# A causal attention layer and a ternary feed-forward layer on one core: own instruction orders for the first two units and the last one, pairwise layer norms, and TensorE transposes of the last unit's probabilities

## What is computed

```python
def _L0_attn_ref(x, W_Q, W_K, W_V, W_O):
    q = jnp.einsum('bsd,hed->bhse', x, W_Q)
    k = jnp.einsum('bsd,hed->bhse', x, W_K)
    v = jnp.einsum('bsd,hed->bhse', x, W_V)
    scores = jnp.einsum('bhse,bhme->bhsm', q, k) * scale
    scores = jnp.where(causal, jnp.float32(-1000000000.0), scores)
    pattern = jax.nn.softmax(scores, axis=-1)
    z = jnp.einsum('bhsm,bhme->bhse', pattern, v)
    out = jnp.einsum('bhse,hde->bsd', z, W_O)
    return out
...
        scale = jnp.mean(jnp.abs(w))
        return jnp.clip(jnp.round(w / (scale + Q_EPS)), -1.0, 1.0)
...
    xn = layernorm(x, ln_gamma, ln_beta)
    w_q = ternary_quantize(weight)
    return jnp.einsum('bsi,oi->bso', xn, w_q) + bias
...
x = x + _L0_attn_ref(_layernorm(x, axis=-1), L0_attn_W_Q, L0_attn_W_K, L0_attn_W_V, L0_attn_W_O)
x = x + _L0_ffn_ref(_layernorm(x, axis=-1), L0_ffn_weight, L0_ffn_bias, L0_ffn_ln_gamma, L0_ffn_ln_beta)
```

## Time and profile before

| what | us |
|---|---|
| median of 3 runs | 897.38 |
| lowest, highest | 896.47, 899.69 |
| profiled execution, device time | 896.73 |
| its span | 894.4 |
| busy PE, DVE, ACT, POOL | 820.2, 673.1, 544.9, 548.8 |

### The profile page before, as it was taken

How to read it: one execution, slowest core, us unless ns; L and a number is a source line. 1 busy time by engine, 2 the same in 40 slices (tenths; PEclk the granted TensorE clock), 3 DMA queues, 4 the chain that set the end, 5 groups by cost and what they waited for, 6 DMA issues and landing times.

```text
span 894.4 us, 14482 instructions
## 1 busy us (share of the span) xinstructions
PE 820.2 (92%) x4790; PEld 731.5 (82%) x4790; DVE 673.1 (75%) x1448; ACT 544.9 (61%) x986; POOL 548.8 (61%) x283
## 2 busy tenths in 40 slices
PE   3879999999999999999999999999999999985264
PEld 3768889899988888888898998888888899974254
DVE  7577787877787787787877787787788777875444
ACT  1456666766666766666766766666667766654300
POOL 5026866677656855696577855684677666644521
PEclk7999999999999999999999999999999999998676
DMA  5045565566556565566555656556456655565011
GB/s 170 1 115 133 131 165 129 134 144 168 132 133 144 141 152 129 121 143 162 132 132 142 168 137 142 124 137 161 115 127 146 143 133 132 133 139 121 21 48 47
DMA packets 58696, 114.62 MB, mean 128 GB/s; under 512 B 17408, under 2 KB 21632, under 8 KB 58624
## 3 DMA queue, kind: packets, MB, share of 16 engines
q1 hardware_dynamic: 58624, 113.71, 53.2%
HBM read 10.88 MB, written 2.10 MB: 15 GB/s over the span
## 4 chain that ended last, share of the span: by engine, by line
PE 79%; DVE 7%; SPq 5%; DMA 3%; ACT 3%; issue 1%; POOL 1%; ACTq 0%; DVEq 0%
PE ring L460 21%; PE scores L498 20%; PE ring L439 17%; PE ring L448 9%; PE ring L469 9%; SPq L316 5%; DMA pT<-turn 3%; DVE norm L728 1%; PE ring L478 1%; DVE stats L710 1%; ACT turn L574 1%; POOL pT L383 1%; DVE scores L656 1%; PE ring L430 1%; ACT pT L594 1%
## 5 line engine op out<-in xcount | busy, mean ns | idle before, releaser
L383 POOL TENSOR_TENSOR pT<-pT 128x1024 fp32r<-128x1024 f32 x192 | 458.4, 2406 | 288.5 <-ACT pT L594 288.1
L656 DVE CUSTOM_DVE_ANT_0 scores<-scores,mask 128x128 f32<-128x128 f32 (+7 forms) x256 | 194.6, 760 | 157.3 <-PE scores L498 155.7
L574 ACT ACTIVATE turn<-scores,negmax 128x128 f32<-128x128 f32 (+7 forms) x256 | 189.4, 740 | 169.0 <-DMA pT<-turn 86.9
L498 PE MATMUL scores<-kT,qT 128*128 128x512 f32 (+3 forms) x1152 | 236.1, 344 | 11.7 <-ACT turn L574 10.1
L460 PE MATMUL ring<-pT,v 128*128 128x512 f32 (+3 forms) x1152 | 223.3, 348 | 9.4 <-POOL pT L383 9.4
L460 PEld LDWEIGHTS ring<-pT,v 128*128 128x128 f32 x1152 | 196.9, 190 | 39.1 <-issue 9.6
L594 ACT ACTIVATE pT<-pT 128x1024 fp32r<-128x1024 f32 x192 | 201.8, 1058 | 24.0 <-DMA pT<-turn 23.0
L498 PEld LDWEIGHTS scores<-kT,qT 128*128 128x128 f32 x1152 | 187.3, 190 | 34.1 <-ACT turn L574 14.1
L664 DVE STREAM_TRANSPOSE turn<-turn 128x128 f32<-128x128 f32 (+7 forms) x256 | 193.9, 768 | 2.3 <-ACT turn L574 2.2
L469 PE MATMUL ring<-wo_s,zT 128*128 128x256 f32 x768 | 114.7, 286 | 0.0
L439 PE MATMUL ring<-xT,wk_s 128*128 128x512 f32 x384 | 102.9, 404 | 8.9 <-DVE xT L752 7.8
(11 more groups left out here) (62 smaller groups left out, 462.7 us busy)
## 6 DMA issues: line engine op xcount, KB each, us to landing
pT<-turn SPq DMA_DIRECT2D x512, 128.0 KB, 2.3
pT<-turn SPq DMA_DIRECT2D x512, 64.0 KB, 2.0
acc<-in_x SPq DMA_DIRECT2D x4, 512.0 KB, 5.8
wq_raw<-in_wq SPq DMA_DIRECT2D x8, 256.0 KB, 3.6
wk_raw<-in_wk SPq DMA_DIRECT2D x8, 256.0 KB, 3.0
...
```

Source lines behind the costliest of these rows:

```text
L383: pool.tensor_tensor(chunk(half, LO, c), f32(chunk(half, LO, c)), f32(chunk(half, HI, c)), ALU.subtract).then_inc(plo_ready, 1)
L498: mm = pe.matmul(scores[:, t % 2, first + c:first + c + n], qT[:, par, a, t * P:(t + 1) * P], kT[:, par, m, c:c + n], start=(i == 0), stop ...
L574: act.activation(turn[half][:, :, 0:t + 1, q, :].rearrange("p b j i -> p j b i"), scores[:, t % 2, score_columns(t)].rearrange("p (j b i) ...
L656: dve.tensor_tensor_reduce(out=tile, in0=tile, in1=mask[:, S - (t + 1) * P:S], scale=-1.0, scalar=FAR, op0=ALU.add, op1=ALU.min, accum_out ...
```

## The change

The tables for the steady part are the same. `stream` is replaced by `run_of`, which runs a start list written out item by item (units 0 and 1), the table for units 2 to 30, and an end list written out item by item (from `pv` of unit 29 on). The rest:

- **Norms by pairs.** x is loaded, and both norms are worked, by pairs of tiles. For the first norm ScalarE writes the normed tiles (`Identity` with scale and bias), for which VectorE makes `-mean*rstd` (`shift`). In the second norm GpSimd writes pairs 0 to 3 and ScalarE pairs 4 to 7. An `x` or `xf` job is the four transposes of a pair. Two `ACT_TABLE_LOAD`s come in on ScalarE around the last exponentials.
- **Start.** GpSimd clears `turn1` before its weight splits and the k weights come first; `qk` 0 of units 0 and 1 are made together; the `wo` load waits for `x` 6 in place of the eighth group of transposes.
- **Last unit (31).** There is no flip, wave, `hip` or `lop`. Its exponentials go to `turn` in plain order (`last_turn`), TensorE transposes them by blocks of 128 x 128 in ten jobs `tp` (`TURNS`, 36 transposes), and ScalarE and VectorE split these into places of `xT`, `v`, `qT` and `kT` that are free by then (`last_probs`). The product with V is three jobs `pvl`, of query tiles 0 to 3, 4 and 5, 6 and 7 (`GROUPS`).
- **Second layer.** The ternary weight is made by GpSimd in three instructions (it was two on VectorE); the bias is added by pairs on GpSimd; `xf` and `ff` go pair by pair between the `o` jobs of unit 31.

```diff
+STEADY_FROM = 2
...
+        yield from start
+        for u in range(STEADY_FROM, LAST):
+            for entry in table:
+                item = entry[:-1] + (u + entry[-1],)
+                if exists(item):
+                    yield item
+        yield from end
...
+            def normalise(item):
+                kind, c = item
+                act.wait_ge(ln_step, ln_no[rstd_of("rstd2" if kind == "norm2" else "rstd", c)])
+                wait_norm_place(act, item)
+                for t in (2 * c, 2 * c + 1):
+                    last = act.activation(norm[:, t % 4, :], acc[:, t, :], ACT.Identity, bias=shift[:, t:t + 1],
+                                          scale=rstd[:, t:t + 1])
+                last.then_inc(norm_by_scalar, 1)
...
-                    sp.wait_ge(job_done, job["x", 12, 4, KD - 1] + 1)
+                    sp.wait_ge(job_done, job["x", NT // 2 - 2] + 1)
                     load(wo_raw, wo[0], wo_in)
...
+            def turn_probs(k, dst):
+                at = 0
+                for t, j0, n in TURNS[k]:
+                    pe.wait_ge(probs_ready, LAST * QT + t + 1)
+                    for j in range(j0, j0 + n):
+                        mm = pe.transpose(dst[:, at * P:(at + 1) * P], last_turn(t)[:, j * P:(j + 1) * P], ident[:, :])
+                        at += 1
+                return mm
...
+            def last_weighted_v(g, dst):
+                first, n = GROUPS[g]
...
+                for j in range(first + n):
...
+                            pe.wait_ge(job_taken, job["tp", k] + 1)
...
+            def ternary_weight():
+                pool.wait_ge(job_taken, job["wsum",] + 1)
+                pool.tensor_scalar(wf_neg, wf_raw, thr[:, 1:2], None, ALU.is_lt).then_inc(tern_step, 1)
+                pool.wait_ge(job_done, last_of("qk", (0, 1), LAST))
+                pool.tensor_scalar(wf_raw, wf_raw, thr[:, 0:1], None, ALU.is_gt).then_inc(tern_step, 1)
+                pool.wait_ge(tern_step, 2)
+                pool.tensor_tensor(wf_s[:, :, :], wf_raw, wf_neg, ALU.subtract).then_inc(wf_ready, 1)
```

597 lines of the change are left out of this document (339 added, 258 removed), and 24 rows, old and new, of tables (END_SCALAR, END_TENSOR, END_VECTOR, START_TENSOR).

## The result

The changed kernel takes 824.47 us, median of 4 runs (823.35 to 826.2), against 897.40 us of the kernel before in the same session (896.47 to 899.69): a ratio of 0.919, 95% interval 0.916 to 0.921. The forecast was 830.0 us, in a range of 819 to 842.

A forecast was written before the change was run, and what follows sets the result against it. TensorE bounds the middle (708.45 us, kept), while chains of waits leave it idle 73 us at the two ends. Span 894.4 - 20.3 (start) - 47.1 (end) = 827.0, plus 2.3 and 0.7 = 830.0 us; 8-in-10 range 819 to 842.

The forecast's parts named there:

- Start, first link: Start: x load, norms and splits by pairs let the first projection begin at 10.0 us and not 19.53.
- Second link: Start: transposes and first products bring the first score tile to 18.7 us; tile 7 is flipped at 36.5, was 58.4.
- Third link: Start: SyncE's second group of waves, behind the `wo` load, at 38.9 us; `pv` of half 1 at 57.5, gain 20.3.
- End, first link: Last stage: unit 31's exponentials wait for unit 30's half 1; the last ends about 814.6 us, was 815.2, nothing gained.
- End, second link: Last stage: VectorE's queue ends last; with 2 us for waits 847.3 us, stage 61.1, gain 47.1, floor 52.5.
- GpSimd: Last stage: normed tiles at 0.77 us, ternary instructions 1.2, a pair's bias 1.3, all hidden by 1 to 7 us.
- Table loads: Two more on ScalarE in the last stage, 1.28 us each; by the skill's drain up to 2.8 us longer, not used.
- rivals, 1: Last stage: GpSimd's normed tiles take 2.5 us each, the end comes 5 to 8 us later, 837 us; chance 0.09.
- Rival 2: Last stage: TensorE runs transposes and products between them at half clock, stage 71 us, total 840 us; chance 0.09.
- Rival 3: Start: the wave queue holds it, SyncE's second group starts at 50 and not 38.9 us, total 841 us; chance 0.06.
- Rival 4: Last stage: denser, near VectorE's floor plus 3 us of lead-in, total 815 to 821 us; chance 0.09.
- Rival 5: Middle: units wait for their waves; 26.8 us a unit would eat both gains, 27.3 gives 912 us; chance 0.01.

The follow-up runs named there:

- 8: Changed kernel with each of the last unit's 36 probability transposes on TensorE done twice: 824.44 us, against 824.47.
- Experiment 5: Changed kernel with the first `wo` load issued behind the first eight waves of each half of unit 0, not ahead of its second group: 819.61 us.
- 6: Changed kernel with the square root of tiles 0 to 7 moved behind the last exponential and the early table load gone: 829.04 us.
- 7: Changed kernel with each of GpSimd's eight normed tiles of the second layer computed twice: 832.48 us.
- 9: On top of Experiment 5, VectorE's reciprocal for the norms of tiles 0 to 7 moved ahead of unit 31's last maximum: 821.99 us.
- 3: Changed kernel with unit 31 turned by flips and DMA waves again, second-layer norms and splits ahead of the half-1 waves: 855.73 us.
- 4: Changed kernel with the second layer of tiles 8 to 15 made in one go behind the last projection: 831.69 us.
- 10: Changed kernel with the last unit's products of query tiles 4 and 5 joined with those of 6 and 7: 829.09 us.
- 11: Changed kernel with unit 31 by waves again, probabilities split on landing, GpSimd's low parts first, all normed tiles on ScalarE: 845.29 us.

## Why the prediction was right, and where it was not

The chain's times of the changed kernel against the sum: `pv(1,0)` at 58.34 for 57.5, the middle 705.82 for 708.45, the end 58.14 for 61.1. The errors are +0.84, -2.63 and -2.96, together the -4.75 between 827.0 and 822.3. What lies outside the span was 2.1 us, and the median lay 0.1 above: 2.2 where I added 3.0. The mechanism was right: TensorE's idle time at the two ends went and the middle stayed. That it came within 5.5 us is in part luck: the terms of the start were 1.7 us too short, and VectorE's work at the end was summed 2.9 us too long. And one of my own signs of being wrong came true: GpSimd ended a wait of TensorE in the last stage.

- **Start, first link: right in kind, 1.7 us short.** The first statistics began at 3.68 us (for 3.7) and a pair on ScalarE took 1.04 (for 0.8 to 0.9). The warm-up ran until 8.22 us, 0.11 us a matmul to the last, and held the first transposes, which I had starting at 7.1; in 8 it ended at 7.2 and the projection began at 10.46. The warm-up is the step that I left out of the sum. The projection ran at half rate, as expected, 2.86 us for 2.9; in seven of the twelve profiles with this start it did not. A small instruction of VectorE beside GpSimd's split, 128 x 4 elements, took 0.69 us and not the 0.16 of its like, and stood in the chain.
- **Second link: right.** First score tile 19.9 us (18.7), the last flip 37.3 (36.5): the lag of the first link and no more. I had counted four jobs of 1.44 us between the first projection and that tile; the list has eight transposes and three jobs, 5.4 us for 5.8.
- **Third link: right on the numbers, and a chance missed.** Second group at 40.08 us for 38.9, and 18.3 us from there to `pv(1,0)` for 17.7. The terms gave 56.6 us, 1.7 too few; the 0.9 that I put on top, for no named cause, covers half. I saw that the `wo` load would hold the queue behind the flips and took it as given. Experiment 5 shows that it need not; the sum's own terms gave 1.9 us for it (38.4 less 36.5), and 1.6 to 2.4 were measured.
- **Middle: -2.6 us.** 1.4 us are a job that moved: `qk` 1 of unit 31 stands ahead of `pv(1,29)` in the table and behind it in the end list. I left it in the 708.45 and took the end's first link from a trace in which it did not stand there, so the total has it once and only the border is wrong. The other 1.2 us go with rarer hold-ups: the chain of before has four pieces in the middle in which a wave took 3.6 to 4.1 us to land, that of the changed kernel one. Nothing was run on that.
- **End, first link: right.** Exponential 4 of unit 31 at 19.3 us behind `pv(1,29)` (18.2, with the moved job not yet in it), the last exponential's end at 29.0 (28.4).
- **End, second link: right path, work summed too high, waits about as allowed.** To the end of the last `o` addition 17.0 us (17.7), behind it 9.5 (10.1), the store 2.7 (2.6). I had 27.8 us of VectorE's work without a wait, and 2 us of waits on top. Measured are 24.9 us of work and 1.6 of waits:

```profile
793.14:819.62 26.48, 24.90 (x69) 1.00 0.17 56
```

  The single rows were close: busy times by form and shape add up to 27.4 us. But an instruction of VectorE begins up to 0.1 us before the one ahead of it ends (802.43 + 0.68 and 803.02), so 69 in a row take 2.5 us less than their sum. The same is wrong in the floor of 52.5 us, which the measured 50.94 undercut. The spell at half clock that the 2 us were to cover as well did not come: TensorE's clock is 1.00 in this stretch. And 845.0 and 2 make 847.0, not 847.3.
- **GpSimd: wrong.** Its normed tile takes 1.23 us and not 0.77, and the second pair was not hidden "by 1 to 7 us" but 1.2 us late; experiments 6 and 7 show the price of more, and 9 the wait gone. The bound of 2.5 covered the tile; the claim of slack rested on taking the two-input bias row as the nearest. The ternary instructions took 1.58, 1.58 and 1.29 us for 1.2 each, the first two just over the upper bound of 1.54. The pair's bias at 1.31 was right.
- **Table loads: right in the trace's price.** Three loads of 1.28 us in ScalarE's last stage, the next instruction at once behind. 6 has none between the exponentials and its last exponential ends 1.1 us earlier, but GpSimd's later start would hide what that gained; what the loads cost in time is not shown.

ScalarE's timeline of the changed kernel around them:

```profile
787.63 1.28 ACT L799 ACT_TABLE_LOAD   x1
788.93 0.30 ACT L799 ACTIVATE std<-mv,consts 128x8 f32<-128x8 f32 x1
...
789.73 1.28 ACT L773 ACT_TABLE_LOAD   x1
791.03 1.01 ACT L773 ACTIVATE turn<-scores,negmax 128x896 f32<-128x896 f32 x1
```

0.02 us lie between a load's end and the next start. The drain of 1.38 us a switch, which the Trainium skill has on its page "ScalarE: Activation LUTs", section "What ACT_TABLE_LOAD costs", does not appear as a gap here, neither ahead of the loads nor behind them.

Of the rivals, 1 was off in the tile's time and, by 7, near in its price, in part by a clock that it did not have. Rival 2, by the rule of the Trainium skill's page "TensorE: Matmul & The Clock Gate", section "Part 4: PE-mode transpose", did not come: eleven transposes took 1.36 us at a granted clock of 1.00, even 36 more of them (8) left the stage there. Its sum was wrong as well: half of 50 us at half rate makes 75 us, not 62.

```profile
799.97 1.36 PE L602 MATMUL ring<-ident,turn 128*128 128x128 f32 x11
```
```profile
761.12:821.80 60.68, 56.05 (x403) 52.11 (x401) 52.21 (x137) 40.24 (x80) 38.35 (x25) 1.00 0.31 83
```

The trace does not bear the rule out for f32 transposes between products. Where TensorE did run at half rate in the last stage (3, 4, 6, 7, 10 and 11), it was behind waits that the experiments put in. Rival 3 named the right place; at 1.2 us it was not a case of its own. Rival 4 is half true: the stage took 58.1 us, between the forecast's 61.1 and the 55.5 of that rival, since VectorE's floor was summed too high. Rival 5 is refuted in each of the thirteen kernels by its middle. Not run one by one are the items of the start's order, GpSimd's ternary weight and the bias by pairs.
